# A sequence memory layer with expert routing: its interleaving string written anew, four row scatters in one step

## The chip, the cores and the metric

One core of a Trainium2 chip runs the whole program. The metric is the device time of one execution in microseconds (us), lower is better. The engines are PE (TensorE), DVE (VectorE), ACT (ScalarE), POOL (GpSimd) and SP (SyncE, which here only starts transfers). Each engine works through its own instruction queue strictly in the order in which the program wrote it; engines meet through semaphores.

## The reference

Inputs: hidden is 16 sequences of 512 tokens of 256 features. A memory of two 64x64 matrices per sequence is learnt over four chunks of 128 tokens, then every token goes through one of 8 experts.

```python
# attention part, per chunk of 128 tokens
k, v, q = conv4(hidden @ Wk.T), conv4(hidden @ Wv.T), conv4(hidden @ Wq.T)
g = grad(sum((silu(k @ W1.T) @ W2.T - v)**2)) * 0.1      # at the chunk's start state, clipped to norm 1
S = eta_t * S - theta_t * g_t ;  W = (1 - alpha_t) * W + S    # scan over the tokens
out = (silu(q @ W1_t.T) @ W2_t.T) @ Wo.T
out = out * rsqrt(mean(out*out) + 1e-6) * norm_g * (hidden @ gW.T + gb)
x = layernorm(hidden + out)
# expert part
chosen = argmax(x @ gate_w.T)                             # one of 8 experts a token
x = layernorm(x + (x + x @ expert_w[chosen].T))
```

(The kernel adds 2 on the diagonal of each expert's weights, so that one product gives the whole sum under the last layer norm.)

## The kernel before

The 16 sequences are handled four at a time (G = 4 groups), and the 512 positions in four chunks (NC = 4). So the first part has 16 instances, numbered 0 to f, each of 128 positions by four sequences. Every instance goes through five stages, written as Python generators: `project` (p: projections, gates, the convolution), `respond` (s: decay factors, the k-q products), `learn` (l: gradients and their norm), `retrieve` (r: outputs, state update) and `epilogue` (e: output norm, residual, layer norm, routing). Every `yield` ends one step of a stage.

The epilogue is the one that matters here. Its steps are: e.0 the product with `w_o` (L924); e.1 the root mean square on POOL (L935, L937); e.2 the gated product into `y` on DVE (L941); e.3 a POOL transfer that adds `hidden` onto `y` in place (L947, "y load" below); e.4 layer norm statistics on DVE (L952, L957) and the inverse deviation on POOL (L959 to L964); e.5 the normed rows on ACT (L970); then routing scores (L977 to L1010), the position of each row among the rows of its expert (L1017 to L1027, with the running count `routed` on POOL, L1025), the row index (L1031, L1033), and four indirect transfers of POOL that scatter 128 rows each into `sorted_rows`, grouped by expert (L1037).

The second part works on the sorted rows. From the counts a table of tiles is computed, in three parts (`table`, steps y, m and z): 40 tiles once 12 instances are routed, 8 tiles once 14 are, 24 tiles once all 16 are. The third table first writes eight padding tiles, by eight value loads and transfers on SP (L1097, L1098). Tiles go in 36 pairs through `experts` (x): `load` (SP, L1215 and L1220), `turn` (PE transposes, L1229), `scale`, `multiply` (PE, L1252, with statistics on DVE, L1256) and `send` (ACT L1286, then two indirect transfers of POOL into `out`, L1291). Multiply runs one pair behind load, scale and send two behind. The load of pair 20 waits for the second table, the load of pair 24 for the third. The weights w are loaded in steps w0.

What sets the order of every engine's queue is one string, `ORDER`: two characters name a generator, and the program calls `next` on it. Step after step, the instructions of that step are appended to the queues of their engines. Nothing is reordered later.

Of the kernel before, what the change touches and what calls it, by code (L numbers as in the profile page):

```python
# [34 lines left out]
G = 4  # L35
NB = B // G
# [32 lines left out]
class Counts:  # L69
# [79 lines left out]
def build(nc, dram):  # L149
    out = dram["out"]  # L150
    with ExitStack() as ctx:
# [193 lines left out]
        nc.vector.wait_ge(s_prep, n_bias)  # L345

        layers(nc, ctx, sb, sem, dict(locals()))


def layers(nc, ctx, sb, sem, v):  # L350
# [12 lines left out]
    pe, act, dve, pool, sp = nc.tensor, nc.scalar, nc.vector, nc.gpsimd, nc.sync  # L363
# [72 lines left out]
    s_scatter = [sem(f"s_scatter{i}") for i in range(2)]  # L436
# [471 lines left out]
        rtv.freed_by(i, n("w2_t"))  # L908
        yield

    def scattered_before(c, g):

        return 16 + (c * (G // 2) + g // 2) * NB * 16

    def epilogue(c, g):

        n, o, o2, p = names(c, g)
        i2 = g % 2
# [385 lines left out]
    for letter, stage in dict(p=project, s=respond, l=learn, r=retrieve, e=epilogue).items():  # L1304
        steps.update({f"{letter}{n:x}": stage(n // G, n % G) for n in range(NC * G)})
# [6 lines left out]


ORDER = (
    "p0p0p0p2p0p0p0p0p1p0p1p1p1p0p1p1p0p1p1s0l0p1s0p1p0p1l0p1l0s0l0s0l0s0l0s1l0p2s1l0l0s1s1p2s1l0l1s0p2r0l1p2s0r0l1l1p2p2r0s1"
    "p2p2l1l1l1p2p3p2s2r0l1l1l2e0r0l2e0e0s2s1l2e0p3p3s2l1p3s2p3e0p3p3p3p3p3p3r1p5r1e0p4l2s2r1l2e0p3s2l2s3p6l2l2e0r0s3s3p4l2p4"
    "p4s3p4s3p4e0l2e0p4p4e0l3r1r1r2e1e0s3l3l3e1s2p4r2r2l3s4e1p4r1l3l3s4s4e0e1p5l3s4s3l3p5p5s4p5p5l3p5e0p5l4l3e1p4r2e0p5p5p5l4"
    "s4l4r3l4e2r2l4e2r3p5r3l4l4s5e1e0s5s5e0e2p6l4p6p6p6l4l5p6p6p7e2r3e0p6l4p6e1p6e1p6e2r2l5l5r4e1e1s5s4r3l5s6e2e1s5e3l5e1r4e1"
    "s6l5p7e3s6l5e3s5p7p7p7l5r4e2p7p7e3p7p7l5l6r3l5e1e1e2s6p7e1p8s5p7l6r4s6l6e1e2e2r5l6p9e1e3r4e4p7l6e2l6p8l6e4r5s7e3p8p8s7e2"
    "l6l6s6e2e4l7r5e2e2p8e4p8l6p8p8l7e3p8e3r5par6e3s7e3e2s6e2s7e2l7r5r4l7s8r6e5e4e3s7e3l7l7s8e5e4pbl7r6p9e5p9l7p9s8e3p9s7p8e5"  # L1320
    "p9p9p8l7p9e4l8p9l7p9e3p9e4e3pdl8r6s8e4s7r7e4e3e3e5s9l8e3l8r6e6r7s9e6l8e4r5s9e4pap9l8r7l8e5e4s8s8l8l8pae6l9r6pae4l8papar7"
    "e5l9e6e4papal9r7s9e5l9e4s9e5r8e5l9s8e4l9s9e5pae4e6e7sae7r8sae6l9l9r8e5pal9e7sapbpapbe5lae6pbsalal9e5lae5pbpbpbr8pbe6lar7"
    "pbpbe6pce5e7e6s9sapbe6r9e8e5e6lar8lasapbsbe5e7e7lar9sbsbe8lapce6r9e8pclapce6e6pcr9lbe6pcpcpce7pclblbe8e7lae6lbe7e7pclbr8"
    "e6sae8rasclblbsbe8lbe9sbe7e7r9lbpdpdpde9rae7e9sbpfe7e7rapdpdpde9e7pdlce8lbpde8ralclcpce8sbe8rbe7e8e7lce8e8pde8pdlclcpee8"
    "e9sdeascscralcear9rbe9pepdpelcsceasdlcrbsde9sdeapescpee9e8ldsce8rbe9e8e9earcldpepeebpee9eae9e9ebldrbldebpercebralde9e9ld"
    "ealdrclepee9ealeseldeae9rcseeae9eaebsdseecebseldeaealepfececpfpfsdeaeasepfrdpfebealepfpfebleleebecrbebw0seebleebeaeaebrd"
    "pfleperdebebpfpfy0rdedebpfecy0y0sfy0sfy0leecy0ededebresflfecsfeclfebececlfeclfececlfw0edecx0ecedecsfx0x0ecw0x0lfrerelfed"
    "x0lfy0x0x0ecx0rex0lfsfx0x0x0x0eeeex0x0x0x0eex0x0x0x0x0x0x0eeedx0x0x0x0x0x0x0x0x0edx0edx0edx0x0x0edededx0edx0x0rfeem0x0x0"
    "x0x0edeerfx0rfeeedrfedx0x0x0x0x0x0x0m0efx0edefx0x0efx0x0efm0x0x0x0eex0x0x0eex0m0x0eeeex0x0x0x0efx0x0x0x0eex0x0eex0x0x0ef"
    "x0x0eem0x0x0x0m0efx0x0efx0x0efx0x0x0efx0x0efeeefefx0eeefm0eex0x0efx0efefx0z0efx0eez0x0x0x0x0x0x0x0x0x0z0z0x0x0z0z0x0z0x0"  # L1330
    "z0x0x0x0x0x0x0x0x0x0x0x0x0x0x0x0x0x0x0x0x0x0x0x0x0x0x0x0x0x0x0x0x0x0x0x0x0x0x0x0x0x0x0x0x0x0x0x0x0x0x0x0x0x0x0x0x0x0x0x0"
    "x0x0x0x0x0x0x0x0x0"
)


# [45 lines left out]
```

## Time and profile before

| | us |
|---|---|
| median of 3 runs | 543.25 (542.83 to 543.25) |
| the profiled execution | 543.25 |
| its span, first to last instruction | 542.0 |
| PE, DVE, ACT, POOL busy | 451.1, 386.2, 311.1, 337.5 |
| POOL, indirect transfers L1037 and L1291 | 75.0 and 70.3 |
| mean granted TensorE clock | 0.936 of full speed |

The page is read from the stretches first: which engine is full there, and which wait ends last. The busy share over the whole span mixes the first part (up to about 400 us) with the second.

### The profile page before, as it was taken

The page shows a single profiled execution, that of the slowest core. Times are in us where ns is not written, and L with a number is a line of the kernel's source. Part 1 is how long each engine was busy: PE and PEld are TensorE (multiplying, and loading weights), DVE is VectorE, ACT ScalarE, POOL GpSimd, SP SyncE. Part 2 cuts the span into 40 slices and gives each one's busy share as a digit, 9 for nine tenths or more (in the row PEclk, how much of TensorE's full clock was granted, in tenths as well). Part 3 has the DMA queues.
Part 4 walks back from the last instruction along what each step waited for, and adds up shares of the span by engine and source line. Part 5 has one row for each costly group of instructions (what it writes and reads, how often), then busy time and mean ns, then how long its engine had stood idle before and what let it go on. Part 6 is the DMA issues. An engine that isn't in the chain of part 4 may idle for free.

```text
span 542.0 us, 11153 instructions
## 1 busy us (share of the span) xinstructions
PE 451.1 (83%) x3502; PEld 339.2 (63%) x3502; DVE 386.2 (71%) x1123; ACT 311.1 (57%) x779; POOL 337.5 (62%) x451
## 2 busy tenths in 40 slices
PE   4788798999989888988989789978669778773991
PEld 2465665867857666765758376747458667652880
DVE  3387787996988689779965697976896637444572
ACT  1445366477486647566744567646447766732772
POOL 2005445458676845868656769676547768775677
PEclk9899899999999999999989899998589989877997
DMA  8432435444645264445356255454775566436641
GB/s 220 142 99 65 114 70 138 119 103 125 158 94 160 65 178 104 120 97 148 79 149 142 65 166 110 111 166 102 240 179 158 152 182 194 143 115 220 194 156 61
DMA packets 61354, 73.21 MB, mean 135 GB/s; under 512 B 17293, under 2 KB 48206, under 8 KB 61296
## 3 DMA queue, kind: packets, MB, share of 16 engines
q1 hardware_dynamic: 50624, 46.12, 30.9%
q0 software_dynamic: 8848, 25.44, 17.4%
q10 hardware_dynamic: 1824, 0.93, 0.6%
q8 instruction: 29, 0.48, 0.4%
q14 instruction: 29, 0.24, 0.2%
HBM read 44.19 MB, written 19.22 MB: 117 GB/s over the span
## 4 chain that ended last, share of the span: by engine, by line
PE 31%; POOL 18%; DVE 17%; issue 12%; DMA 10%; ACT 7%; SPq 4%; POOLq 0%; DVEq 0%; ACTq 0%
PE bank L1252 7%; DMA y<-in_hidden 6%; DVE kq_in L559 4%; PE bank L518 3%; ACT rows L970 3%; POOL sorted_rows L1037 3%; POOL rstd L962 2%; PE bank L605 2%; POOL out L1291 2%; POOL ab_h L850 2%; PE bank L536 2%; DVE y L941 2%; PE bank L924 2%; PE bank L1229 2%; PE both L1252 2%
## 5 line engine op out<-in xcount | busy, mean ns | idle before, releaser
L1037 POOL DMA_INDIRECT sorted_rows<-rows,index x64 | 75.0, 1172 | 27.5 <-POOL index L1033 13.5
L1291 POOL DMA_INDIRECT out<-os,xs_token x71 | 70.3, 990 | 30.9 <-issue 12.9
L518 PE MATMUL bank<-front 128*64 128x256 f32 x512 | 67.1, 417 | 16.8 <-DMA bias_t<-in_bias_t 7.4
L559 DVE SCALAR_TENSOR_TENSOR kq_in<-shared,conv_w,kq_in 128x256 f32<-128x256 f32 x144 | 70.9, 548 | 11.0 <-ACT kq_in L553 10.7
L518 PEld LDWEIGHTS bank<-front 128*64 128x64 f32 x512 | 38.7, 149 | 39.4 <-issue 8.8
L605 PE MATMUL bank<-front 128*128 128x256 f32 x256 | 60.5, 383 | 0.9 <-ACT shared L524 0.9
L1252 PE MATMUL bank<-shared,front 128*128 x220 | 58.9, 415 | 2.1 <-issue 1.2
L605 PEld LDWEIGHTS bank<-front 128*128 128x128 f32 x256 | 46.7, 190 | 8.8 <-ACT shared L524 1.7
L1252 PEld LDWEIGHTS bank<-shared,front 128*128 128x128 f32 x220 | 43.4, 208 | 10.6 <-issue 4.9
L970 ACT ACTIVATE rows<-y,rstd 128x256 f32<-128x256 f32 x64 | 33.1, 589 | 23.3 <-POOL rstd L964 19.7
L941 DVE SCALAR_TENSOR_TENSOR y<-bank,rms,gt 128x256 f32<-128x256 f32 x64 | 26.5, 475 | 20.0 <-ACT rows L971 10.1
L1286 ACT ACTIVATE os<-bank,rs 128x256 f32<-128x256 f32 x55 | 28.1, 561 | 17.9 <-DVE rs L1275 12.8
L536 PE MATMUL bank<-front 128*128 128x512 f32 x64 | 32.0, 623 | 0.9 <-DVE kq L690 0.5
L850 POOL TENSOR_TENSOR ab_h<-hq,carry 128x512 f32<-128x512 f32 x13 | 19.3, 1484 | 21.1 <-DMA hq<-hq 21.0
L1256 DVE BATCH_NORM_STATS2 st<-bank 128x6 f32<-128x256 f32 x55 | 21.0, 422 | 14.8 <-PE bank L1252 14.4
L952 DVE BATCH_NORM_STATS2 stats<-y 128x6 f32<-128x256 f32 x64 | 22.3, 410 | 11.7 <-DMA y<-in_hidden 11.7
L931 ACT ACTIVATE junk<-bank 128x256 f32<-128x256 f32 x64 | 24.5, 383 | 10.7 <-PE bank L924 9.0
L797 POOL TENSOR_TENSOR small<-norms 128x8 f32<-128x8 f32 x16 | 6.4, 402 | 37.2 <-DVE norms L793 36.8
L609 DVE TENSOR_TENSOR gt<-bank,bias_g 128x512 f32<-128x512 f32 x32 | 21.4, 679 | 8.6 <-PE bank L605 8.6
L1273 DVE RECIPROCAL rs<-rs 128x2 f32<-128x2 f32 (+1 forms) x36 | 5.9, 163 | 27.9 <-ACT rs L1271 27.8
L553 ACT ACTIVATE kq_in<-shared,conv_b,conv_w 128x256 f32<-128x256 f32 x48 | 25.2, 595 | 0.0
L977 PE MATMUL bank<-ident,rows 128*128 128x128 f32 x128 | 19.4, 297 | 6.5 <-ACT rows L971 3.0
(213 smaller groups left out, 1202.3 us busy)
## 6 DMA issues: line engine op xcount, KB each, us to landing
front<-sorted_rows SPq DMA_DIRECT2D x71, 130.0 KB, 2.4
front<-in_hidden_t SPq DMA_DIRECT2D x16, 512.0 KB
decay<-gate_clear SPq DMA_DIRECT2D x16, 512.0 KB, 4.3
y<-in_hidden POOLq DMA_DIRECT2D x16, 512.0 KB
q<-kq_in SPq DMA_DIRECT2D x64, 64.0 KB, 2.5
carry<-carry_rows SPq DMA_DIRECT2D x32, 128.0 KB, 2.8
hq<-hq SPq DMA_DIRECT2D x64, 64.0 KB
shared<-in_w_expert SPq DMA_DIRECT2D x2, 1024.0 KB, 8.8
```

Of the source, the lines that this page charges most:

```text
L518: ins = pe.matmul(halves[half(side), kind, :, :], w[:, k, kind * D:(kind + 1) * D], pairs[:, k, side, :, :], start=k == 0, stop=k == KH - 1)
L536: ins = pe.matmul(bank[:, :], w_ae[:, k, :], xt[:, k, :], start=k == 0, stop=k == KH - 1)
L553: act.activation(kq_in[i2][:, kind, :, :], raw[g][:, kind, :, 0:P], ACT.Identity, bias=conv_b[:, kind:kind + 1], scale=conv_w[:, kind, 0:1]))
L559: dve.scalar_tensor_tensor(dst, raw[g][:, kind, :, tap:tap + P], conv_w[:, kind, tap:tap + 1], dst, ALU.mult, ALU.add))
L605: ins = pe.matmul(bank[:, (b % 2) * H:(b % 2 + 1) * H], xt[:, k, b * P:(b + 1) * P], w_g[:, k, :], start=k == 0, stop=k == KH - 1)
L850: mark(who, n("ab_h"), wide_e.tensor_tensor(ab_h[:, :, :], hq2[:, :, :], carry[i2][:, :, :], ALU.mult))
L941: mark("dve", n(f"gated{b}"), dve.scalar_tensor_tensor(Y[:, b, :], wo[b], rms[:, 1, b:b + 1], gt[g][:, b, 0:H], ALU.mult, ALU.mult))
L970: act.activation(R[:, b, 0:H], Y[:, b, :], ACT.Identity, bias=rstd[:, 2, b:b + 1], scale=rstd[:, 1, b:b + 1])
L1037: pool.indirect_dma_start(sorted_rows[:, :], bass.IndirectOffsetOnAxis(index[i2][:, b:b + 1], 0), R[:, b, :], None, bounds_check=NE * REGI ...
L1252: ins = pe.matmul(both[:, i, :], xs_t[t % TURNED][:, i, k, :], w_expert[:, k, bass.ds(expert, 1), :], start=k == 0, stop=k == KH - 1)
L1286: act.activation(os_[o][:, i, :], both[:, i, :], ACT.Identity, bias=rs[o][:, 2, i:i + 1], scale=rs[o][:, 1, i:i + 1]))
L1291: pool.indirect_dma_start(out[:, :], bass.IndirectOffsetOnAxis(xs_token[t % LOADS][:, i:i + 1], 0), os_[o][:, i, :], None, bounds_check=TO ...
```

## The change

The string `ORDER` is written anew over the whole program, and the four scatters of an epilogue form one step in place of four (the `yield` moves out of the loop), so nothing can stand between them in any queue. The string has 981 steps in place of 1029, which is 3 fewer for each of the 16 epilogues. The count that ACT waits for before it overwrites `rows` has the same value, written in place. The instructions are the same ones on every engine, and as many; only the 20 activation table loads of ACT fall partly at other places. Lines of the new program after L910 have numbers 4 lower.

```diff
-    def scattered_before(c, g):
-
-        return 16 + (c * (G // 2) + g // 2) * NB * 16
-
...
-        act.wait_ge(s_scatter[i2], scattered_before(c, g))
+        act.wait_ge(s_scatter[i2], c * (2 * NB * 16) + (g // 2) * NB * 16 + 16)
...
         for b in range(NB):
             pool.indirect_dma_start(sorted_rows[:, :], bass.IndirectOffsetOnAxis(index[i2][:, b:b + 1], 0), R[:, b, :], None,
                                     bounds_check=NE * REGION - 1, oob_is_err=False).then_inc(s_scatter[i2], 16)
-            yield
+        yield
...
 ORDER = (
-    "p0p0p0p2p0p0p0p0p1p0p1p1p1p0p1p1p0p1p1s0l0p1s0p1p0p1l0p1l0s0l0s0l0s0l0s1l0p2s1l0l0s1s1p2s1l0l1s0p2r0l1p2s0r0l1l1p2p2r0s1"
...
+    "p0p0p0p0p0p1p0p0p0p0s0p1p1p1p0p1p1p1p0p1l0p1p1l0l0p3p1s0l0s0l0l0p1p2l0l0s1s1s0s0l0s1l1l0s0p2p2p2r0p2p2p2p2r0r0l1p2p2l1r0"
```

**The end of the first part, on POOL.** Before, the queue from a little ahead of the routing of instance e to its end:

```order
L1291 DMA out<-os,xs_token 8192x256 x4
L1025 TENSOR_TENSOR routed<-routed,onehot 128x32
L1291 DMA out<-os,xs_token 8192x256 x4
L1033 CAST index<-where_f 128x4
L1037 DMA sorted_rows<-rows,index 66688x260 x2
L1025 TENSOR_TENSOR routed<-routed,onehot 128x32
L1037 DMA sorted_rows<-rows,index 66688x260
L1291 DMA out<-os,xs_token 8192x256 x2
L1033 CAST index<-where_f 128x4
L1037 DMA sorted_rows<-rows,index 66688x260 x5
L1291 DMA out<-os,xs_token 8192x256 x35
```

The same place now (L1021, L1029, L1033, L1287 are the former L1025, L1033, L1037, L1291):

```order
L1287 DMA out<-os,xs_token 8192x256 x8
L1021 TENSOR_TENSOR routed<-routed,onehot 128x32
L1287 DMA out<-os,xs_token 8192x256 x2
L1029 CAST index<-where_f 128x4
L1033 DMA sorted_rows<-rows,index 66688x260 x4
L1021 TENSOR_TENSOR routed<-routed,onehot 128x32
L1287 DMA out<-os,xs_token 8192x256 x4
L1029 CAST index<-where_f 128x4
L1033 DMA sorted_rows<-rows,index 66688x260 x4
L1287 DMA out<-os,xs_token 8192x256 x41
```

Of the 71 output scatters, 34 stood ahead of the last routing count before and 26 do now; of the 64 row scatters, 58 before and 60 now.

**Around a y load, on POOL.** Before, at the ninth of the 16 y loads (its instruction is L947, now L943):

```order
L1025 TENSOR_TENSOR routed<-routed,onehot 128x32
L1033 CAST index<-where_f 128x4
L1037 DMA sorted_rows<-rows,index 66688x260 x2
L947 DMA y<-in_hidden 128x1024
L812 TENSOR_TENSOR small<-small,theta 128x4
L1037 DMA sorted_rows<-rows,index 66688x260 x2
L715 TENSOR_TENSOR ck<-k_n,resp 128x512
L959 TENSOR_SCALAR rstd<-mv 128x4
```

Now, at the ninth:

```order
L943 DMA y<-in_hidden 128x1024
L812 TENSOR_TENSOR small<-small,theta 128x4
L1021 TENSOR_TENSOR routed<-routed,onehot 128x32
L715 TENSOR_TENSOR ck<-k_n,resp 128x512
L1029 CAST index<-where_f 128x4
L1033 DMA sorted_rows<-rows,index 66688x260 x4
L955 TENSOR_SCALAR rstd<-mv 128x4
```

The y load moved from between the scatters of the instance before to ahead of all four. In the new order none of the first 13 y loads has a scatter directly ahead of it.

**The start, on PE.** Before:

```order
L518 MATMUL bank<-front 64x256 x16
L536 MATMUL bank<-front 128x512 x2
L568 MATMUL bank<-front,mask_ae 32x128 x4
L518 MATMUL bank<-front 64x256 x16
L536 MATMUL bank<-front 128x512 x2
L605 MATMUL bank<-front 128x256 x8
```

Now:

```order
L518 MATMUL bank<-front 64x256 x16
L536 MATMUL bank<-front 128x512 x2
L568 MATMUL bank<-front,mask_ae 32x128 x4
L605 MATMUL bank<-front 128x256 x4
L644 MATMUL bank<-ident,kq_in 128x128 x2
L518 MATMUL bank<-front 64x256 x16
```

Half of the gate product of instance 0 (L605) moved ahead of the projections of instance 1 (the second L518).

## Rows read from the trace of the kernel before

**Rows 1.** The page, busy time of each engine over the span.

```profile
PE 451.1 (83%) x3502; PEld 339.2 (63%) x3502; DVE 386.2 (71%) x1123; ACT 311.1 (57%) x779; POOL 337.5 (62%) x451
```

**Rows 2.** Stretches: length, busy (x) of PE PEld DVE ACT POOL, PEclk, DMA share, GB/s.

```profile
80.00:360.00 280.00, 255.61 (x2266) 190.34 (x2262) 227.01 (x525) 172.92 (x457) 192.00 (x262) 0.99 0.48 125
...
400.00:480.00 80.00, 64.15 (x432) 50.79 (x430) 48.02 (x227) 53.33 (x126) 59.15 (x75) 0.93 0.56 166
```

**Rows 3.** POOL in order of time: start, length, instruction [idle before <-releaser].

```profile
479.28 0.26 POOL L1025 TENSOR_TENSOR routed<-routed,onehot 128x32 bf16<-128x32 bf16 x1
...
497.31 0.97 POOL L1291 DMA_INDIRECT out<-os,xs_token  x1 [0.30 <-issue]
502.75 0.97 POOL L1291 DMA_INDIRECT out<-os,xs_token  x1 [4.47 <-ACT os L1286]
...
506.65 0.97 POOL L1291 DMA_INDIRECT out<-os,xs_token  x1 [1.66 <-DVE mvs L1261]
...
539.87 0.97 POOL L1291 DMA_INDIRECT out<-os,xs_token  x1 [0.30 <-issue]
```

**Rows 4.** PE and SP's queue in order of time, the third table and after.

```profile
479.60 0.27 PE L1080 MATMUL bank<-routed,ones_bf 128*128 128x8 bf16 x4 [1.73 <-POOL routed L1025]
...
486.64 8.48 SPq L1098 DMA_DIRECT2D sorted_rows<-pad_row  x8
...
495.87 4.45 SPq L1220 DMA_DIRECT2D front<-sorted_rows  x6
...
498.59 1.11 PE L1229 MATMUL both<-ident,front 128*128 128x128 f32 x4 [8.94 <-DMA front<-sorted_rows]
```

**Rows 5.** Chain that ended last, products of pairs: start us, us, what.

```profile
510.34 1.73 PE bank L1252 x8
512.07 0.44 PE bank L1229 x4
```

**Rows 6.** PE and DVE in order of time, the start.

```profile
16.25 0.43 PE L568 MATMUL bank<-front,mask_ae 128*32 128x128 f32 x8 [1.04 <-ACT front L541]
18.61 5.36 PE L518 MATMUL bank<-front 128*64 128x256 f32 x32 [1.94 <-DMA front<-in_hidden_t]
...
20.94 0.41 DVE L324 TENSOR_TENSOR bias_g<-bias_g,norm_g 128x256 f32<-128x256 f32 x1
```

**Rows 7.** Groups of instructions by line: shapes xcount | busy us, mean ns | idle before.

```profile
L680 DVE TENSOR_TENSOR_SCAN resp<-decay,resp 128x512 f32<-128x512 f32 x16 | 20.4, 1273 | 0.1
...
L690 DVE TENSOR_TENSOR kq<-bank,resp 128x256 f32<-128x256 f32 x32 | 11.9, 412 | 1.3 <-PE bank L686 1.2
```

**Rows 8.** Chain that ended last: the y loads on it, from issue to landing.

```profile
137.53 5.58 DMA y<-in_hidden
...
265.55 9.48 DMA y<-in_hidden
...
289.58 9.10 DMA y<-in_hidden
...
349.06 8.34 DMA y<-in_hidden
```

**Rows 9.** Waits: engine, line, whom it waited for: us in total, times, longest.

```profile
POOL rstd L959 <- DVE mv L957: 23.0, 7, 5.8
...
DVE stats L952 <- DMA y<-in_hidden: 11.7, 5, 5.3
```

**Rows 10.** POOL in order of time: scatters ahead of three of these y loads.

```profile
264.23 1.32 POOL L1037 DMA_INDIRECT sorted_rows<-rows,index  x1 [0.18 <-issue]
...
288.04 1.56 POOL L1037 DMA_INDIRECT sorted_rows<-rows,index  x1 [0.30 <-issue]
...
340.49 0.97 POOL L1037 DMA_INDIRECT sorted_rows<-rows,index  x1 [0.30 <-issue]
```

More of the change, by code:

```diff
@@ L1314 @@
 ORDER = (
-    "p0p0p0p2p0p0p0p0p1p0p1p1p1p0p1p1p0p1p1s0l0p1s0p1p0p1l0p1l0s0l0s0l0s0l0s1l0p2s1l0l0s1s1p2s1l0l1s0p2r0l1p2s0r0l1l1p2p2r0s1"
-    "p2p2l1l1l1p2p3p2s2r0l1l1l2e0r0l2e0e0s2s1l2e0p3p3s2l1p3s2p3e0p3p3p3p3p3p3r1p5r1e0p4l2s2r1l2e0p3s2l2s3p6l2l2e0r0s3s3p4l2p4"
-    "p4s3p4s3p4e0l2e0p4p4e0l3r1r1r2e1e0s3l3l3e1s2p4r2r2l3s4e1p4r1l3l3s4s4e0e1p5l3s4s3l3p5p5s4p5p5l3p5e0p5l4l3e1p4r2e0p5p5p5l4"
-    "s4l4r3l4e2r2l4e2r3p5r3l4l4s5e1e0s5s5e0e2p6l4p6p6p6l4l5p6p6p7e2r3e0p6l4p6e1p6e1p6e2r2l5l5r4e1e1s5s4r3l5s6e2e1s5e3l5e1r4e1"
@@ L1319 @@
[L1319 to L1330, printed above, removed]
@@ L1331 @@
-    "z0x0x0x0x0x0x0x0x0x0x0x0x0x0x0x0x0x0x0x0x0x0x0x0x0x0x0x0x0x0x0x0x0x0x0x0x0x0x0x0x0x0x0x0x0x0x0x0x0x0x0x0x0x0x0x0x0x0x0x0"
-    "x0x0x0x0x0x0x0x0x0"
+    "p0p0p0p0p0p1p0p0p0p0s0p1p1p1p0p1p1p1p0p1l0p1p1l0l0p3p1s0l0s0l0l0p1p2l0l0s1s1s0s0l0s1l1l0s0p2p2p2r0p2p2p2p2r0r0l1p2p2l1r0"
+    "p2l1s1s1l1s0e0s1e0l1s2s1l1e0l1l1s2l2r0s2s2e0l1p3p3p3p3p3e0p3p3p3p3p3r1l2r0e0r1l2s2l2p4s3r1e0l2s2e0p3l2p5s3p4s3p4p4l2e0l2"
+    "l2e0p4l2p4p4p4r1p4l3s2r2p4p4e0l3s3l3e0s3e1p6l3e1r1e0l3s4s3r2s4l3r2l3s4e1l3l3l4e1p5s3p5s4p5s4e0p5p5l3p5p5r1r2s4l4l4p5p5p5"
@@ new lines @@
+    "l4r3e2r2p5e1l4r3e2l4s5s5l4l4s5e1r3p6e2p6p6l4e2p6r3p6l4p6p6e0l5p7e1s4s5p6p6l5e1r4l5l5e2s6r3e1l5r2r4e1l5l5e3s5r4p7e2s6s6p7"
+    "e3l5p7e3p7p7l5e3p7r4p7e1l6p6e1e1l5e2s5p7e2p7s5p7e1e2e2e1l6e2l6r5l6e4r4e3l6r3p7l6p8r5s6e3l6s7e4p8e2l6s7p8s7e4l6p8s6r5p8s6"
+    "pbe2p8e4p8p8pal6e3l7p8e2p8e2l7r6s7e3s6r5l7l7e3e3p9p8r5e5e4s7s8e3r4e5r6l7l7s8l7p9e3e3l7e4p9p9l7e5p9l8r6e3l7p9p9p9p9e5s7l8"
+    "p9l8p9l8e3e4s8r7r6e4l8l8e4r6e4e5s7e6p9l8r5r7e6s9e4e5e4pas8pas9e6pas8l8r7pae4pal8pal8e6pae5l9pae4pal9e5l9s8s8r7e5e5e4l9e6"
@@ new lines @@
+    "r8s9pcs9l9e7r7r6l9sar8e6pbl9pbpbe7sae7l9e5l9s9s9r8e7pbpbl9pbs9pbe6lae5r8e6pbe5pbe6e5pae5e7e6pbe6lalar9lasbr8e6lalae8e7pb"
+    "r7sasae8r9e6lasbpce8pclapcsalar9pcpcpcpclbsae7pce7pdsbr8lbe7e8lblae6sae7e6pce7sbr9rae7lbr9e8pflbscrasce9e9sce8rae7sbsclb"
+    "pdpcsbpdlbpde9pdralbpdpde9pde8pdlblce8lbpdpde7sblclce7pee8rblce8rar9pde9lclceae8scsdldlcrbsde9e8sdpeeaeapepelce8rbpelcsd"
+    "scpesdpepee9rbealde8e9e8ldrcldsde9e9eapepelde9ebldebrbealde9selde9pfrcpfebebeasepfldseeae9e9rceapfeaebpfeapfpfrcseraecec"
@@ new lines @@
+    "rdw0leeaebpfleeaecpfeaecealeleseebrdleleebpesfseleebleebebebebrbrdpfebebeclfrdy0edpfy0lfsfy0y0y0lelfecedsfy0reedlfw0sfec"
+    "x0lfrereececlfecrex0x0eeedw0edsfsfx0lfx0eeedx0eclfx0y0eex0eeecx0eclfx0x0x0x0x0ecx0x0x0x0ecx0x0x0rfeex0x0x0edrfedx0rfx0ed"
+    "ededrfedededx0edx0efx0efx0x0x0x0eex0efefx0x0x0x0x0x0x0x0x0eex0x0x0x0x0x0efeem0x0x0x0x0x0eex0m0eex0x0x0efx0eex0m0m0x0x0ee"
+    "eex0x0efx0x0x0eex0x0x0m0efeex0x0efm0efefx0efefx0efx0m0x0x0x0x0x0x0x0z0x0z0x0efx0x0x0x0x0x0x0x0x0x0x0x0x0x0x0x0x0z0z0z0z0"
@@ L1333 @@
+    "z0x0z0x0x0x0x0x0x0x0x0x0x0x0x0x0x0x0x0x0x0x0x0x0x0x0x0x0x0x0x0x0x0x0x0x0x0x0x0x0x0x0x0x0x0x0x0x0x0x0x0x0x0x0x0x0x0x0x0x0"
+    "x0x0x0x0x0x0x0x0x0x0x0x0x0x0x0x0x0x0x0x0x0"
 )
```

## The prediction, made before the changed kernel ran

> **What bounds the kernel now.** I read the page's busy times first, then the stretches, then the waits, then the chain. Over the span no engine is full, PE 83% and POOL 62% [rows 1], but that mean hides two regimes. From 80 to 360 us PE is busy 255.6 of 280 us at a granted clock of 0.99 [rows 2]: the first part is PE's, with 24.4 us of holes. After 400 us it is POOL's. POOL shows only 59.2 busy us of 80 there [rows 2], but each indirect scatter shows 0.97 us and is followed by 0.30 in which POOL waits for nothing, so one scatter occupies 1.28 us. From 506.65 to 539.87 there are 27 scatters, 26 intervals of 1.28 = 33.2 us, without a hole [rows 3]; PE needs only 2.17 us for a pair there (1.73 + 0.44) [rows 5] where POOL needs 2 x 1.28 = 2.56.
>
> The end is a chain with a hole in it. The last routing count is done at 479.54 [rows 3], PE counts the tiles at 479.60, SP writes eight padding tiles (486.64 to 495.12), only then issues the next loads (495.87), and the data is there at 498.59 [rows 4], 19.0 us after the count. PE stood for 8.94 us for it [rows 4]. POOL ran dry for 4.47 us and again for 1.66 [rows 3]; less the usual 0.30 each that is 5.5 us in which the engine that bounds the second part did nothing.
>
> **The change, part by part.** The merged step and the literal count emit nothing by themselves; what counts is where instructions now stand.
>
> *The end.* Ahead of the last routing count there are 8 output scatters fewer and 2 row scatters more. If POOL is full up to there, the count is done (8 - 2) x 1.28 = 7.7 us earlier. Behind it stand now 4 row scatters and 71 - 26 = 45 output scatters, 49 x 1.28 = 62.7 us, and about 1.0 for the index and the wait behind it: 63.7. Before, it was 6 + 37 = 43 scatters, 55.0 us, 1.0 and the holes of 5.5, which makes 61.5, and the trace has 540.84 - 479.28 = 61.6 [rows 3]. So the tail gets 2.1 us longer, and starts 7.7 earlier: -5.6. Is there enough POOL work to cover the 19 us of the padding chain? PE's transposes of a pair whose load stands behind the padding block the queue; that was pair 23 and is now pair 22, so output leaves freely up to pair 19: 14 output and 4 row scatters, 23.0 + 1.0 = 24.0 us. The next pair's rows came 502.75 - 479.28 = 23.5 us after the count [rows 3]. Just enough, with a second hole of about 0.8 left. PE has 15 pairs after the padding where it had 14, 2.17 us more, which POOL's 2.56 a pair covers. The tail's term is -4.8. Its bounds: 0 if the count comes only as much earlier as the tail is longer, and -7.7 if also the second table's loads flow better.
>
> *The start.* PE finished the gate matmuls of instance 0 at 16.68 and started the projections of instance 1 at 18.61. Now half of the gate product stands ahead of these, and it needs weights that DVE has ready at 20.94 + 0.41 = 21.35 [rows 6]. PE then stands 4.7 us instead of 1.9: +2.7. Against that, DVE's queue ahead of the first norms is about 2.1 us shorter (the two k-q products, 0.41 each, and the second decay scan, 1.27, stand behind it now [rows 7]). I take +0.7; bounds -2.1 and +2.7.
>
> *The y loads.* Four of them are on the chain, 5.58, 9.48, 9.10 and 8.34 us [rows 8], and DVE stood 11.7 us for such loads in all [rows 9]. The two longest were issued directly behind two scatters (264.23, 288.04), the fourth with the last one 8.6 us back (340.49) [rows 10]. In the new order the load goes first. I give the two longest the time of the unhindered fourth: 9.48 - 8.34 + 9.10 - 8.34 = -1.9. Bounds: 0, if the landing is set by other traffic, and -10.2, if all three longer ones fall to 5.58.
>
> The Trainium skill speaks to this (DMA: Bandwidth & Descriptors, Queues, rings and completion order): a DMA engine takes turns between its queues and works through one queue's ring in order, which it says of the hardware queues. By that the loads would gain, as in rival 1; the row of 349.06, long with nothing ahead, does not bear it out.
>
> *Four scatters in a row.* They hold POOL for 4 x 1.28 = 5.1 us, where before mostly two stood together. Directly behind the block stands in 8 of the first 12 instances the inverse deviation of the next one (L959), and POOL waited for its input anyway, 23.0 us in 7 waits [rows 9], so there the block lies in a wait. In the four others (instances 0, 2, 7 and a) it is the halo copy, an update product or the norm chain that waits up to 2 x 1.28 = 2.6 us longer. I take one of the four as reaching PE: +2.6; bounds 0 and +10.2. The rest of the first part I cost at nothing: per instance the queue of work ahead of each stage differs by a few us in both directions, and cover is what it has: in the 280 us PE has 24.4 of holes [rows 2].
>
> The sum: -4.8 + 0.7 - 1.9 + 2.6 = -3.4. The profiled execution took 543.25 at a span of 542.0, 1.25 outside, and equals the median. So 543.25 - 3.4 = 539.9, a span of 538.6.
>
> **The rivals.** *1, faster still: the y loads.* If a load ahead of the scatters lands in 5.58 like the shortest, the term is -10.2 in place of -1.9, and the four scatters behind it fill the wait of L959 (then the +2.6 falls too): -4.8 + 0.7 - 10.2 = -14.3, 529.0; with half of it reaching PE, 534. For: DVE's 11.7 us and POOL's 23.0 [rows 9]. Against: DVE is not full in the first part, 227.0 of 280 [rows 2], so much of it costs nothing.
>
> *2, slower: the block of four in the first part.* The place is POOL between 80 and 360 us, where it shows 192.0 busy us of 280 [rows 2] and every scatter hides a further 0.30. If an operation that PE waits for (the gradient weight, the carried products) stands 2.6 us longer behind the block in four instances, that is +10.2 in place of +2.6: 547.5. It decides from (3.4 + 2.6) / 2.56, more than two instances. A block also delays the next y load's gated product. Against: most blocks are followed by an operation that waits anyway.
>
> *3, no change.* POOL is not full before the last count (it had waits there too), so the count comes only 2 to 3 us earlier, the tail's 2.1 us more work takes that back, and what is left is the start and one block: 543.
>
> *4, the string does not bring the count forward.* An epilogue's long chain (ACT, PE, DVE, POOL) could be late for another reason, for instance because PE and ACT are given less pair work to cover it; then 49 scatters stand behind an unchanged moment: 543.25 + 2.1 + 0.7 = 546.
>
> **How the numbers follow.** The forecast, 537 to 542, has 0.42; rival 1 has 0.18; rival 2 has 0.16; rival 3 has 0.14; rival 4 has 0.10. A measurement here can tell about 0.2%, that is 1.1 us. Faster than 542.2: 0.42 + 0.18, less 0.02 at the edge, and 0.01 of rival 3: 0.59. Within: 0.15. Slower than 544.3: 0.26. The range runs from 532, which keeps rival 1 at half of its price, to 548, which keeps rivals 2 and 4; outside stays about 0.1 on each side. The likeliest case's own range is 537 to 542.
>
> **What would show it.** The tail: the last routed count (now L1021) about 66 us before the end of the span, near 473, and no hole above 2 us on POOL behind it. PE's wait for the loads behind the padding still there, 4 to 9 us. The start: PE's second projections at 23 to 24 us. The y loads: no piece above 8.5 us in the chain before 360, and DVE's total wait for them under 8 us. Four in a row: POOL's blocks of 5.1 us, with PE's busy time from 80 to 360 still near 255 of 280. The forecast is wrong if the last count is not before 477, or if the table for pair 0 (first L1229, at 402.76 before) comes more than 3 us later.

## The result, and the profile after

The changed kernel takes 545.66 us (median; 540.12 to 551.37) where the kernel before takes 540.97; the ratio is 1.0074, 95% interval 1.0047 to 1.0099. It is slower by 0.7%, and the forecast of 539.9 had the wrong sign. A second measurement, below, gives 1.011 (1.0048 to 1.0171). Here and below a median is of all runs, while a ratio is of the fast runs alone (those at most about 1.5% above the fastest of their kernel), so a ratio is not quite that of the two medians beside it. The profile shown here is from the second measurement: an execution of 546.40 us with a span of 545.2. The profile of the first one has a span of 578.0 us, with stalls in its second part like those told of below; only its first part is used.

Over the span the page reads almost as before [rows 1]:

```profile
PE 448.3 (82%) x3502; PEld 339.2 (62%) x3502; DVE 380.6 (70%) x1123; ACT 308.9 (57%) x779; POOL 325.2 (60%) x451
```

The stretches (length, busy of PE, PEld, DVE, ACT, POOL, granted clock, DMA share, GB/s), against [rows 2]:

```profile
15.00:30.00 15.00, 9.64 (x55) 6.21 (x56) 5.84 (x14) 4.09 (x10) 0.00 (x0) 0.77 0.30 106
35.00:55.00 20.00, 16.57 (x108) 10.90 (x107) 13.88 (x25) 10.20 (x22) 6.81 (x8) 0.83 0.31 93
80.00:360.00 280.00, 254.29 (x2229) 190.97 (x2225) 222.43 (x519) 171.64 (x450) 179.76 (x256) 0.97 0.47 122
400.00:480.00 80.00, 60.87 (x430) 48.03 (x428) 46.26 (x213) 47.78 (x115) 51.85 (x69) 0.88 0.60 161
```

The first part looks like that of before: PE 254.3 of 280 us busy. The two new facts stand at either end of it. From 15 to 30 and from 35 to 55 us the granted clock is 0.77 and 0.83, where before it was 0.89 and 0.91. And from 400 to 480 us POOL is busy 51.85 us where it was 59.15.

The start, PE in order of time, against [rows 6]:

```profile
15.52 0.42 PE L568 MATMUL bank<-front,mask_ae 128*32 128x128 f32 x8 [1.04 <-ACT front L541]
20.78 3.57 PE L605 MATMUL bank<-front 128*128 128x256 f32 x8 [4.83 <-DVE bias_g L324]
24.19 0.38 PE L644 MATMUL bank<-ident,kq_in 128*128 128x128 f32 x2
24.50 3.67 PE L518 MATMUL bank<-front 128*64 128x256 f32 x32
...
29.93 1.89 PE L605 MATMUL bank<-front 128*128 128x256 f32 x8
```

PE waits 4.83 us for the gate weights, and then the product itself takes 3.57 us, against 1.89 for the same eight records nine us later. The ratio of the two is that of TensorE's two levels, 1.2 and 2.4 GHz. The second projections start at 24.50, where they had started at 18.61 [rows 6].

The end, POOL and PE, against [rows 3, 4]:

```profile
478.89 0.26 POOL L1021 TENSOR_TENSOR routed<-routed,onehot 128x32 bf16<-128x32 bf16 x1
...
485.71 0.19 POOL L1029 CAST index<-where_f 128x4 int32<-128x4 f32 x1 [1.56 <-DVE where_f L1027]
...
543.07 0.97 POOL L1287 DMA_INDIRECT out<-os,xs_token  x1 [0.31 <-issue]
```

```profile
479.20 0.27 PE L1076 MATMUL bank<-routed,ones_bf 128*128 128x8 bf16 x4 [5.13 <-POOL routed L1021]
...
494.27 0.66 PE L1225 MATMUL bank<-ident,front 128*128 128x128 f32 x4 [0.90 <-DMA front<-sorted_rows]
```

The last count is done at the same moment as before (478.89, before 479.28), and behind it stand more scatters. The holes of 4.47 and 1.66 us are gone; the longest is 1.56. Why the count is not earlier is seen at POOL's first output scatter, before and now:

```profile
413.06 1.47 POOL L1291 DMA_INDIRECT out<-os,xs_token  x1 [0.80 <-DVE xs_token L1265]
```

```profile
419.00 1.48 POOL L1287 DMA_INDIRECT out<-os,xs_token  x1 [0.25 <-issue]
```

From there to the last count POOL has no hole above 1.8 us in either kernel, and that stretch is shorter, 59.9 us where it was 66.2. But it starts 5.9 us later. The first turn of a pair, where the first part hands over, comes 3.4 us later than the 402.76 of before:

```profile
406.18 1.02 PE L1225 MATMUL bank<-ident,front 128*128 128x128 f32 x4 [1.28 <-DMA front<-sorted_rows]
```

### The profile page after: what moved, and what is told of

Its sections match the earlier page's. It is cut to its first block, busy times and chain, and to the rows that moved or that the text cites. A ratio compares the mean times of both kernels' runs of the same rounds, so it can differ in the third digit from the quotient of the medians.

```text
span 578.0 us, 11149 instructions
## 1 busy us (share of the span) xinstructions
PE 458.5 (79%) x3502; PEld 347.1 (60%) x3502; DVE 376.7 (65%) x1123; ACT 309.7 (54%) x779; POOL 326.8 (57%) x451
## 4 chain that ended last, share of the span: by engine, by line
PE 41%; DVE 20%; ACT 11%; issue 10%; POOL 8%; another core or an unknown queue 5%; DMA 3%; SPq 1%; ACTq 0%; POOLq 0%; DVEq 0%
DVE kq_in L559 8%; PE bank L518 6%; PE bank L1248 5%; PE bank L605 4%; POOL sorted_rows L1033 3%; PE bank L536 3%; ACT rows L966 2%; PE bank L920 2%; PE both L1248 2%; ACT os L1282 2%; PE bank L686 2%; DVE gt L609 1%; PE both L886 1%; PE bank L1225 1%
## 5 line engine op out<-in xcount | busy, mean ns | idle before, releaser
L1287 POOL DMA_INDIRECT out<-os,xs_token x71 | 70.1, 988 | 46.0 <-ACT os L1282 26.4
L1033 POOL DMA_INDIRECT sorted_rows<-rows,index x64 | 68.7, 1074 | 30.0 <-issue 16.6
L1248 PE MATMUL bank<-shared,front 128*128 x212 | 60.6, 435 | 27.3 <-ACT rs L1267 8.5
L518 PE MATMUL bank<-front 128*64 128x256 f32 x512 | 64.8, 408 | 13.3 <-DMA bias_t<-in_bias_t 7.7
L559 DVE SCALAR_TENSOR_TENSOR kq_in<-shared,conv_w,kq_in 128x256 f32<-128x256 f32 x144 | 69.0, 536 | 9.5 <-ACT kq_in L553 9.3
L605 PE MATMUL bank<-front 128*128 128x256 f32 x256 | 63.1, 396 | 4.8 <-DVE bias_g L324 4.8
L518 PEld LDWEIGHTS bank<-front 128*64 128x64 f32 x512 | 38.8, 148 | 34.4 <-issue 10.8
L605 PEld LDWEIGHTS bank<-front 128*128 128x128 f32 x256 | 48.2, 196 | 12.7 <-issue 6.6
L1252 DVE BATCH_NORM_STATS2 st<-bank 128x6 f32<-128x256 f32 x53 | 20.2, 421 | 26.3 <-remote 11.9
L1228 ACT ACTIVATE front<-bank 128x512 f32<-128x512 f32 x28 | 16.7, 596 | 35.7 <-remote 24.8
L1248 PE MATMUL both<-shared,front 128*128 x72 | 22.9, 474 | 5.7 <-ACT front L1228 4.7
L850 POOL TENSOR_TENSOR ab_h<-hq,carry 128x512 f32<-128x512 f32 x13 | 17.4, 1340 | 14.8 <-DMA hq<-hq 14.8
L793 DVE TENSOR_REDUCE norms<-sq 128x16 f32<-128x1024 f32 x16 | 19.5, 1216 | 7.3 <-ACT sq L790 5.6
```

The source lines that it names most:

```text
L518: ins = pe.matmul(halves[half(side), kind, :, :], w[:, k, kind * D:(kind + 1) * D], pairs[:, k, side, :, :], start=k == 0, stop=k == KH - 1)
L559: dve.scalar_tensor_tensor(dst, raw[g][:, kind, :, tap:tap + P], conv_w[:, kind, tap:tap + 1], dst, ALU.mult, ALU.add))
L605: ins = pe.matmul(bank[:, (b % 2) * H:(b % 2 + 1) * H], xt[:, k, b * P:(b + 1) * P], w_g[:, k, :], start=k == 0, stop=k == KH - 1)
L1248: ins = pe.matmul(both[:, i, :], xs_t[t % TURNED][:, i, k, :], w_expert[:, k, bass.ds(expert, 1), :], start=k == 0, stop=k == KH - 1)
L1287: pool.indirect_dma_start(out[:, :], bass.IndirectOffsetOnAxis(xs_token[t % LOADS][:, i:i + 1], 0), os_[o][:, i, :], None, bounds_check=TO ...
```

## The experiments

The kernels were measured in five groups, each on one chip beside the kernel before. On the chips of the last three groups the kernel before took 565.5 to 567.4 us in place of 541: there the second part of every profiled kernel had stalls of up to 11.3 us (new_with_filled_start) whose releaser the profile does not know (it calls it "remote"), while the first part ran as elsewhere (first turn of a pair in the changed kernel 405.41 there, 406.18 in the profile above). From these groups I use the ratios with care, and the traces up to the first turn of a pair. Two moments serve as milestones: the second gradient weight (POOL, L812) and the first turn (PE, L1229, in the new numbering L1225).

**Cut at the first pair.** The order of one kernel up to the first step of the pairs, then the steps that are left in the order of the other; the four scatters as adjacent steps.

```diff
-ORDER = (the string of before)
+ORDER = (before up to its first x0) + (the rest, as in the new string)   # h_before_then_new
+ORDER = (new up to its first x0) + (the rest, as in the string of before) # h_new_then_before
```

> The changed kernel unaltered, for a second profile of it (the first one shows a span of 578.0 us, far above its usual time) and for its time beside the hybrids of this call. Theory A (the tail of the new order gains about 5 us, its first part loses about 9): last routing count near 478 us of a span near 544, and first L1225 three or more us later than 402.8. Theory B (the tail gains nothing): last routing count as far from the end as before plus the 2 us of added scatters, at 480 or later.

> The order before up to the first expert load (step x0.0), then the new order for all that is left, four scatters as four steps next to each other. Theory A: 4 to 6 us faster than the kernel before (536). Theory B: within 1 us of it.

> The new order up to the first expert load, then the order before for what is left. Theory A: about 9 us slower than the kernel before (550). Theory B: 4 us slower, as the changed kernel is.

Measured beside before at 540.72: the changed kernel 546.19, ratio 1.011 (1.0048 to 1.0171); the first part of before with the new second part 539.85, 0.9983 (0.995 to 1.0017); the new first part with the old second part 547.96, 1.0159 (1.0111 to 1.0208). So the loss goes with the new first part, 1.6% or 8.6 us with the old second part, and the new second part gives back 0.2% on the old first part and 0.5% on the new one, neither clear of noise (the first interval takes in 1, the other two overlap). Theory A was right for the first part; its 4 to 6 us of gain in the tail did not come. The two hybrids together make 1.4%, the whole change 0.7 to 1.1%: a cut between two orders may have a price of its own, as below, and part of the 8.6 us can be that.

In the profile of h_before_then_new the count stands well ahead, but so does everything. The first turn (PE), then the last count and the last scatter (POOL):

```profile
396.11 1.12 PE L1229 MATMUL bank<-ident,front 128*128 128x128 f32 x4
```

```profile
468.26 0.26 POOL L1025 TENSOR_TENSOR routed<-routed,onehot 128x32 bf16<-128x32 bf16 x1
...
532.41 0.97 POOL L1291 DMA_INDIRECT out<-os,xs_token  x1 [0.30 <-issue]
```

From first turn to count it is 72.2 us here and 72.7 in the changed kernel; in the kernel before 479.28 - 402.76 = 76.5. From the count to the start of the last scatter it is 64.2 in both; before, 539.87 - 479.28 = 60.6. The new second part brings the count 4 us forward and makes what is behind it 3.6 us longer: -0.6 in all, which agrees with 0.9983. And its first turn came 6.7 us earlier than in the profile of before. The queues are the same ones only up to the first load of a pair, but the last gate product of PE, which stands ahead of it, is as much earlier (368.63 against 375.95). On which chip the profile of before was taken is not on record. One execution's milestones must be compared with several of the other kernel.

**The block of four alone.** The order of before, with all four scatters where the first of them stood.

```diff
             pool.indirect_dma_start(sorted_rows[:, :], ...).then_inc(s_scatter[i2], 16)
-            yield
+        yield
...
 ORDER = (the string of before, without the second to fourth scatter step of each instance)
```

> The order before, but the four scatters of each epilogue in one step where the first of them stood; nothing else moves. If four in a row hold the operations behind them on POOL and PE waits for these (rival 2), 2.6 us slower for each instance that reaches PE, 3 to 10 us in all. If the block is covered, within 1 us.

Measured 567.66, ratio 1.0516 (1.0461 to 1.0571): 28 us. The stretch, and the waits in it (engine, line, whom it waited for: us in total, times, longest):

```profile
80.00:360.00 280.00, 246.64 (x2085) 184.37 (x2082) 207.96 (x479) 160.50 (x418) 171.76 (x239) 0.94 0.44 113
```

```profile
PE both L831 <- DVE grad_w L815: 10.1, 2, 5.9
...
DVE grad_w L815 <- POOL small L812: 12.7, 5, 5.3
```

The same two waits in the kernel before, same stretch:

```profile
DVE grad_w L815 <- POOL small L812: 3.6, 4, 1.5
PE both L831 <- DVE grad_w L815: 2.5, 3, 1.4
```

POOL's gradient weight (L812) is 0.41 us of work on average, but DVE's L815 waits for it and PE's L831 for that; 5.1 us of block ahead of it become a hole of 5.9 us on PE. Part of the price is the clock. As an estimate from the rows of the stretch, PE's busy time by the granted clock is 246.6 x 0.94 = 231.8 us of full-speed work, before 255.6 x 0.99 = 253.1. Of the 21 us missing in this stretch 9.0 are more idle time, and 12 are lower clock.

**Which blocks cost.** The same block in two sets of the instances: those between whose scatters POOL's queue had no gradient weight (1, 3, 4, 5, 9, a), and the others of 0 to c (0, 2, 6, 7, 8, b, c). In 2, 6, 7, 8 and b a weight stood between the scatters and is now behind all four. In 0 and c, other than the expectation says, it stood right behind the fourth already; there the block only moves up.

```diff
-ORDER = (the string of before)
+ORDER = (the same, the four scatter steps adjacent in instances 1 3 4 5 9 a)   # block_clear_of_weight
+ORDER = (the same, the four scatter steps adjacent in instances 0 2 6 7 8 b c) # block_ahead_of_weight
```

> The kernel before, with the four row scatters in one block at the place of the first in the instances 1, 3, 4, 5, 9 and a alone: between their scatters POOL's queue had no gradient weight (L812). Theory 'weight' (a block costs where the weight, for which DVE's and then PE's next work waits, is moved behind it): 541 to 545, at most 4 us. Theory 'block' (each costs alike, 28 us over 16 instances): 6 of 16, about 10 us, 551.

> The complement: blocks at the place of the first scatter in the instances 0, 2, 6, 7, 8, b and c, where a gradient weight stood between the scatters and now stands behind all four. Theory 'weight': 560 to 567, nearly all of the 28 us. Theory 'block': 7 of 16, about 12 us, 553. With instances d to f, which neither kernel touches, a rest of up to 4 us may be missing in the sum.

Measured 1.0053 (0.9994 to 1.0113) and 1.042 (1.0365 to 1.0476). So six blocks cost 3 us, possibly nothing, and seven others 24. In the second the wait PE L831 for DVE L815 is 8.2 us in the stretch, longest 5.9; in the first 2.7, longest 1.6. A block is cheap where no weight is pushed behind it; what 0 and c add to the 24 us was not separated. In the new order no weight stands between the four scatters of an instance or directly behind them, and the two waits in the changed kernel, same stretch, are no longer than before:

```profile
PE both L831 <- DVE grad_w L815: 2.2, 2, 1.5
DVE grad_w L815 <- POOL small L812: 0.9, 1, 0.9
```

So what made the block of four dear in the old order is not at work in the new one.

**The blocks of the new order taken apart.** Three other steps between each two scatters, instances 0 to c. These steps don't always put something on POOL: in instances 3 and a its queue still has all four together.

```diff
-    "...p6p6p6e0l5p7e1s4s5p6p6l5e1r4..."
+    "...p6p6p6e0l5p7e1e0s4s5p6e0p6l5e1e0r4..."
```

> The new order, but in instances 0 to c the four row scatters are four steps again with three other steps between each two, so that POOL's queue has no block of four there; the rest of the string is as in the changed kernel. Theory 'block' (the 8.7 us that the new first part costs are POOL's blocks of 5.1 us): they come back, 537 to 540 us, ratio to before 0.994 to 0.999. Theory 'order' (the loss is where the stages of the five generators now stand to one another, the blocks lie in waits): 545 to 547, ratio 1.008 to 1.013. In between, say 542 to 544, both carry a part.

Measured 561.77, ratio 1.0369 (1.031 to 1.0429): 20 us slower than before, and 15 more than the changed kernel. Not even the direction of theory "block" came out. But the run has a price of its own, so it does not say what the blocks themselves cost. The wait that grew most is on ACT, over the span:

```profile
ACT rows L970 <- DMA sorted_rows<-rows,index: 28.6, 7, 6.0
```

The changed kernel has 2.3 us there, in one wait. ACT may overwrite `rows` only when the scatters of two instances earlier have landed; a last scatter 9 steps later becomes a wait of up to 6 us in ACT's queue. That these waits make up the whole 15 us was not shown.

**The block at the last scatter's place**, in the order of before, and **the y loads first**: each of the six y loads that had row scatters right ahead of it (instances 4, 7, 8, 9, c, d) moved ahead of them.

```diff
-ORDER = (the string of before)
+ORDER = (the same, scatters 1 to 3 of instances 0 to c moved down to the fourth) # before_block_last
+ORDER = (the same, steps e.3 of 4 7 8 9 c d moved up ahead of the scatters)       # before_y_loads_first
```

> The kernel before, with the four scatters of an instance in one block where the last of them stood (instances 0 to c), so none stands earlier than it did. The block at the place of the first cost 28 us. Theory 'block' (four in a row, 5.1 us of POOL, delay whatever is behind): 550 or more here too. Theory 'place' (scatters moved ahead of the operations that PE waits for, the gradient weight above all, are what cost; at the last place those operations are served earlier than before): 538 to 544.

> The kernel before, with the y load moved ahead of the row scatters in the six instances where some stood right ahead of it (4, 7, 8, 9, c, d). My term: -1.9 us, 539 against 541. Rival 1 (such loads land in 5.58 us): up to -10, 531 to 535. Theory 'hidden or set by other traffic': 540.5 to 541.5.

The block at the last place: 620.37 against 567.37, ratio 1.0978 (1.0897 to 1.106). Theory "place" falls; "block" had the direction, but neither of my theories has room for 53 us in 13 instances: moving scatters down is no safer than moving them up. In its profile ACT stood 33.9 us for POOL's inverse deviation (L964), where it had stood 19.7 before, and DVE 29.8 for ACT's rows, where it had stood 10.1. I did not separate these further.

The y loads: 568.78 against 567.37, ratio 1.0068 (1.0026 to 1.011). Not faster; the first turn came at 400.88, between the 396.11 and 402.76 that the unmoved order showed. In the chain that ended last before 400 us there is one y load left:

```profile
344.64 9.28 DMA y<-in_hidden
```

It is nearly as long as the longest of [rows 8], though the last scatter ahead of it started 8.6 us earlier (336.09). And in h_before_then_new, with the y loads unmoved, the pieces of 9.48 and 9.10 us are not on the chain at all, and DVE's wait for the loads is 3.7 us in place of 11.7 [rows 9]; with the loads moved it is 3.3:

```profile
67.47 6.07 DMA y<-in_hidden
133.51 5.55 DMA y<-in_hidden
342.00 8.85 DMA y<-in_hidden
```

```profile
DVE stats L952 <- DMA y<-in_hidden: 3.7, 3, 2.6
```

What I had read as a property of the order was one of one execution.

**Cuts inside the first part.** New to before at the y load of instance 2 (138 us in the changed kernel) and of instance 7 (262 us there, 266 before; the expectations put these some 30 to 40 us too early), and the complement of the second.

```diff
-ORDER = (the string of before)
+ORDER = (new up to e2's step e.3) + (the rest, as before)    # new_start_then_before
+ORDER = (new up to e7's step e.3) + (the rest, as before)    # new_to_middle_then_before
+ORDER = (before up to e7's step e.3) + (the rest, as in new) # before_to_middle_then_new
```

> The new order up to the y load of instance 2 (about 100 us), then the order of before for all steps that are left, scatters as single steps. If the start (half of the gate product ahead of the second projections) costs what I had as its upper bound, 2.7 us: 543.5 against some 540.8 of before. If the start is free and the loss lies later: 540 to 541.5. If the early instances carry most of the 8.7 us: 546 or more.

> The new order up to the y load of instance 7 (about 235 us), then the order of before. Loss spread evenly over the instances: about 4 us, 545. All in the first half: 548 to 550, as for the cut at the end of the first part (547.96). All in the second half: 540.5 to 541.5.

> The complement: the order of before up to the y load of instance 7, then the new order with the scatters as four adjacent steps. Additive theory: the three add up, so this is 546.2 minus what the cut at the same place costs: 542 if the loss is spread evenly, 537 to 539 if it is all in the first half, 545 to 547 if it is all in the second half.

Measured 1.0143 (1.009 to 1.0196), 1.0081 (1.0044 to 1.0119) and 1.0077 (1.0023 to 1.0131). These don't add up: the shortest new piece costs no less than the longer one, and the two complements cost 0.8% each, together more than the whole change (0.7 to 1.1%). A cut leaves the generators at other distances to one another than either order has, so it has a price of its own, which I cannot take out. What can be read from these traces is what lies before the cut. The second gradient weight, POOL, in the changed kernel, and in h_before_then_new:

```profile
72.86 1.01 POOL L812 TENSOR_TENSOR small<-small,theta 128x4 f32<-128x4 f32 x1
```

```profile
68.18 1.35 POOL L812 TENSOR_TENSOR small<-small,theta 128x4 f32<-128x4 f32 x1
```

Over all profiles of this study with the new start as it is (7) it comes at 72.9 to 74.7, mean 73.9; over all with the old start (11) at 68.2 to 72.0, mean 70.2. The ranges don't meet. Up to there the start costs 3.7 us, and it is the start alone: three of the eleven are the new order with only the start as before (next), at 68.88, 70.37 and 71.05.

**The old start in the new order.** Both halves of instance 0's gate product, and its key transposes, behind the projections of instance 1 again; all else as in the changed kernel.

```diff
-    "p0p0p0p0p0p1p0p0p0p0s0p1p1p1p0p1p1p1p0p1l0p1p1l0l0p3p1..."
+    "p0p0p0p0p0p1p0p0p0p1p1p1p0p0p1p1p1p0p1s0l0p1p1l0l0p3p1..."
```

> The changed kernel with one place of the start as before: both halves of instance 0's gate product, and its key transposes, stand behind the projections of instance 1 again; everything from there on is the new order. Theory 'start' (PE's hole of 4.8 us ahead of the gate product, and the stretches at a granted clock of 0.6 to 0.8 at 20 to 25 and at 40 to 50 us that all new starts show and the old ones mostly do not, cost about 4 us): 541.5 to 543 against 546 of the changed kernel and 541 of before. Theory 'start is covered' (the sum of the prediction, +0.7): 545 to 546.5.

> The same kernel as in new_with_old_start (the changed kernel, with both halves of instance 0's gate product and its key transposes behind the projections of instance 1 again). There the first part ended 5.0 us earlier than in the changed kernel's profile (first turn of a pair 401.17 against 406.18), but the second part of all kernels was slowed on that chip. Theory 'start': 541 to 543 where before takes 541, ratio 1.000 to 1.004. Theory 'the start is one of several equal parts': 544 or more, ratio 1.006 or more.

> The changed kernel with the old start (as new_with_old_start), now beside the changed kernel on one chip. Theory 'start': 4 to 6 us faster than the changed kernel beside it, as the first turn of a pair stood in the traces (400.1 and 401.2 against 406.2). Theory 'swallowed behind the first part': less than 2 us of difference.

> The changed kernel itself, beside old_start_beside. On a chip with before at 541: 1.007 to 1.011 of before. On a chip that slows the second part (before at 566): the old-start form was 1.013 and 1.019 there; if the new start costs its 5 us there too, 1.022 to 1.028.

All four on chips with the disturbed second part: 1.0129 (1.0072 to 1.0187), 1.0188 (1.0139 to 1.0236), 1.0214 (1.0127 to 1.03), and the changed kernel beside the last 1.0253 (1.0101 to 1.0404). Side by side the old start is faster by the ratios by 0.4% or 2.2 us, less than the 4 to 6 expected, and the intervals overlap; the medians of all runs, 576.17 against 580.83, differ by 4.7. So the time does not show the start's price. The traces of the first part show it. The stretches of the start (15 to 30 and 35 to 55 us), and the first turn, from new_with_old_start_again:

```profile
15.00:30.00 15.00, 13.12 (x83) 8.24 (x82) 7.93 (x19) 8.60 (x20) 0.00 (x0) 1.00 0.29 98
35.00:55.00 20.00, 18.18 (x114) 12.24 (x114) 13.86 (x25) 9.10 (x21) 7.01 (x9) 0.83 0.33 90
```

```profile
400.07 0.66 PE L1225 MATMUL bank<-ident,front 128*128 128x128 f32 x4 [1.58 <-DMA front<-sorted_rows]
```

(From 35 to 55 us the clock is at 0.83 here too, so that stretch is no mark of the new start. From 15 to 30 us it is 0.77 in all seven profiles with the new start, and 0.89 to 1.00 in eleven of the twelve with the old one.) First turns: with the new start and the whole new first part 405.38, 405.41, 406.18 and 407.74 (mean 406.2); with the old start 400.07, 401.17 and 404.18 (401.8); in the order of before 396.11 and 402.76 (399.4). Of the 6.8 us between the first and the last mean, the start has 4.4. The other 2.4 are less than the spread of one order's own executions.

**The hole at the start filled.** Four idle products of 512 columns ahead of the gate product, in the changed kernel; and, in h_before_then_new, one ahead of the projections of instance 1 and three of 256 columns ahead of the first theta product. They write banks that the next product overwrites, and change nothing in the output.

```diff
+            if c == 0 and g == 0 and two_of == 0:
+                for _ in range(4):
+                    pe.matmul(bank[:, :], w_ae[:, 0, :], xt[:, 0, :], start=True, stop=True)
+                all_ready(pe)
```

> The changed kernel with four idle products of 512 columns (about 1 us each) into the bank that the gate product then overwrites, issued in PE's hole ahead of it; they add nothing to the output, and the hole keeps its length. If the price of the new start is the granted clock behind the hole: the clock at 20 to 25 us stays at 1.0, the gate product's first four take 1.9 in place of 3.6 us, and the kernel is 1.7 us faster, 544 to 544.5, or 3 to 4 faster where the second low stretch at 40 to 50 goes with it. If the clock is no cause: 545.5 to 546.5.

> The order of before up to the first pair, then the new order (539.85 on its first chip, ratio 0.998), and idle products in two of PE's holes of the start: one of 512 columns ahead of the projections of instance 1, three of 256 ahead of the first theta product. They add nothing to the output. If low granted clock at 15 to 50 us (1.6 to 4.3 us lost there in the profiles of the old start) is a cause: 2 us earlier at the first weights, 537 to 538.5, ratio 0.993 to 0.996. If what is gained at the start is swallowed later: 539.5 to 541, ratio 0.997 to 1.000. If the idle products themselves delay PE: above 541.

The filled start of the changed kernel, PE:

```profile
17.41 0.43 PE L568 MATMUL bank<-front,mask_ae 128*32 128x128 f32 x8 [1.04 <-ACT front L541]
17.77 3.70 PE L604 MATMUL bank<-front 128*128 128x512 f32 x8
22.67 1.97 PE L608 MATMUL bank<-front 128*128 128x256 f32 x8 [1.20 <-DVE bias_g L324]
```

The gate product takes 1.97 us in place of 3.57, as expected: the low clock was behind the hole, and goes with it. (The Trainium skill, TensorE: Matmul & The Clock Gate, Part 1, has TensorE at half rate by default and after idleness, and at full rate once it is kept busy; this row agrees.) The second gradient weight comes at 72.90 and the first turn at 404.82, hardly earlier than in the changed kernel. But this execution was 1.9 us behind already ahead of the hole (L568 at 17.41, above at 15.52). Counted from L568 the second weight comes after 55.5 us; in the seven profiles with the new start after 57.3 to 57.9, mean 57.7; in the eleven with the old one after 51.2 to 56.6, mean 53.2. So in this one execution the filled hole gives back 2.2 of the 4.4 us that the new start costs up to there. The time, 574.14 against 567.37, 1.0158 (1.0083 to 1.0234), decides nothing on that chip. The filled form of h_before_then_new gave 1.0127 (1.0073 to 1.0181) there, although its first part was early (first turn 399.08), so it does not show a gain either. No kernel that I ran is shown to be faster than before; h_before_then_new, at 0.9983, is the nearest.

## Why the prediction was wrong, point by point

The measured 545.66 lies between the outer ends that I gave, 532 and 548, but only because these kept rivals 2 and 4; the likeliest case, 537 to 542, failed, in its direction and in its two main terms.

**The start, +0.7 with bounds -2.1 and +2.7, measured +3.7 in the traces.** The wait was right: 4.7 us said, 4.83 in the trace, and the second projections at 24.50 where I said 23 to 24. Two things failed. I costed the wait and not what follows it: the half gate product ran at 1.2 GHz and took 1.6 to 1.7 us more, and the filled hole gave back 2.2 us. And I let 2.1 us of a shorter DVE queue pay for the wait; up to the second gradient weight nothing of it is to be seen. The term lies outside its bounds.

**The end, -4.8, measured about -0.6.** The step that failed is "if POOL is full up to there". It is full only from its first output scatter on. That stretch became 6.3 us shorter (59.9 for 66.2), near the 7.7 that I gave. But it starts 5.9 us later: 3.4 because the first turn is later, and 2.5 because between the first turn and the first output scatter POOL now waits for the epilogue's chain. Before, four row scatters stood there (401.41 to 412.03); now they stand behind that scatter, and in their place is a wait:

```profile
407.42 0.22 POOL L955 TENSOR_SCALAR rstd<-mv 128x4 f32<-128x4 f32 x1 [7.94 <-DVE mv L953]
```

So the count came 4 us earlier relative to the first turn and not 7.7. The other side of the term held: behind the count 3.6 us more, where I had 2.1 and a hole of 0.8; POOL full to the end; the count 66 us before the end of the span (545.2 - 478.9 = 66.3). PE's wait behind the padding, for which I gave 4 to 9 us, is 0.90. PE had waited 5.13 for the count instead and still had pairs in hand.

**The y loads, -1.9, no gain measured.** Both tests I had named came out (no piece above 8.5 us before 360, though one of 9.25 at 375.31; DVE's wait 2.2 us), and still no gain was found: a second execution of the old order has neither the two long pieces nor the long wait, and the loads moved by themselves made nothing faster (1.0068). It was a term made of one execution's chain. Rival 1, built on the same rows, falls with it.

**Four in a row, +2.6.** I did not measure the term by itself. The mechanism of rival 2 is real, and far dearer than I priced it where nothing else moves: 28 us, not 10, because the weight's wait reaches PE and the clock falls behind the hole. But the new order does not suffer from that: no weight stands right behind its blocks, and PE's wait for it is 2.2 us where it was 2.5. PE's busy time from 80 to 360 is 254.3, near 255 as said, and with the y loads at 0 the other 2.4 us of the first part would fit +2.6, though they cannot be told from chance.

**The sum.** With the measured terms it is +3.7 or +4.4 (start) + 2.4 (rest of the first part, uncertain) - 0.6 (end) = +5.5 to +6.2; measured +4.0 to +5.9. Both conditions under which I called the forecast wrong came true: the last count at 478.89, not before 477, and the first turn 3.4 us later. The tail by itself came out as in rival 3: a count some 4 us earlier, and as much more work behind it. The total looks like rival 4, a count that is not brought forward, at 546, but most of what stands in place of its cause, an epilogue short of cover, is the start.

**Open.** On the chips with the disturbed second part, kernels with the new second part were 1.3 to 2.1% slower than before even where they had the old start or the whole old first part. The waits that those profiles call "remote" are longer with the new second part: on DVE 23.1 to 34.4 us in seven profiles, against 8.2 to 11.9 in four with the old one; on ACT 27.2 to 35.2 against 15.4 to 26.2. So it seems to suffer more from these stalls; why, and from what in it, was not tried. What the new start costs in the kernel's time, and not only in the traces of the first part, was not measured on a chip without those stalls; and what the other 2.4 us of the first part are, if anything, is not known.

## What to carry to other kernels

Price a hole on TensorE at its length plus the work behind it at half clock, and don't let another engine's shorter queue pay for it. Before scatters are moved in a strict queue, look for the short operation behind them that a chain waits for (here a weight of 0.41 us) and for the buffer that their landing frees: too early and too late both cost several per cent. A term read from the waits or the chain of one execution wants a second execution before it is counted.

## What the runs showed of the hardware

Two profiled executions of one and the same instruction order differ by several us in the first part alone (last gate product 368.63 and 375.95; first turn 396.11 and 402.76). Part of this is the granted clock at the start: 1.00 from 15 to 30 us in the one, 0.89 in the other, and PE's second projections took 3.67 us behind a wait for their load of 0.58 in the one, and 5.36 behind one of 1.94 in the other [rows 6]. All twelve profiles in which these projections come first show the same: seven with a wait of 0.28 to 1.18 us took 3.67 us at a clock of 1.00, five with one of 1.42 to 2.60 us took 4.99 to 6.36 at 0.77 to 0.89. In each, PE had already waited about 1 us just before, ahead of L568. The rows of the first:

```profile
15.00:30.00 15.00, 12.89 (x84) 8.37 (x83) 9.38 (x23) 8.42 (x20) 0.00 (x0) 1.00 0.24 91
```

```profile
17.93 3.67 PE L518 MATMUL bank<-front 128*64 128x256 f32 x32 [0.58 <-DMA front<-in_hidden_t]
```

(both from h_before_then_new). And chips differ: the same kernel before took 541 us in the first measurement and in two groups, and 565.5 to 567.4 in the three groups on other chips. The kernel before was not profiled there; in the kernels that were, all of the stalls but single ones of at most 4.5 us stand behind the first turn of a pair.
